# A graph-masked transformer block: the transposes in front of the MLP leave TensorE and take the way through 32x32 blocks and HBM

## The reference

```
nx = ln(x, ln1_g, ln1_b)
q, k, v = nx @ wq + bq, nx @ wk + bk, nx @ wv + bv        # 8 heads of 32
bias = where(adj > 0, 0.1 * adj * adj, -inf)
attn = softmax(q @ k.T / sqrt(32) + bias)                  # per head, 128x128
x1 = x + (attn @ v) @ wo + bo
n2 = ln(x1, ln2_g, ln2_b)
out = x1 + gelu(n2 @ w1 + b1) @ w2 + b2                    # 256 -> 1024 -> 256
```

## Time and profile before

| | |
|---|---|
| median of 3 runs | 1369.9 us |
| profiled execution, its own time | 1371.92 us |
| its span, first to last instruction | 1370.1 us |
| mean granted TensorE clock | 0.979 |
| PE, PEld busy | 97%, 84% |
| ACT, DVE, POOL busy | 84%, 83%, 47% |
| DMA | 155 GB/s, 212.80 MB |

### The profile page before, as it was taken

One profiled execution on the slowest core, in us unless ns is written; L12 is line 12 of the kernel. 1 busy time (PEld: TensorE's weight loads), 2 busy tenths in 40 slices (PEclk: granted clock), 3 DMA queues, 4 the chain that ended last, 5 costly groups with the idle time before them and its releaser, 6 DMA issues.

```text
span 1370.1 us, 33628 instructions
## 1 busy us (share of the span) xinstructions
PE 1333.6 (97%) x11364; PEld 1147.1 (84%) x11364; DVE 1140.7 (83%) x1971; ACT 1151.4 (84%) x3336; POOL 642.1 (47%) x615
## 2 busy tenths in 40 slices
PE   8579999999999999999999999999999999999999
PEld 7458888888888888888888888888888888888878
DVE  4789888888888888888888888888888888898762
ACT  4569888889888888988888988898988888898763
POOL 5634445554455554454555445555445455444110
PEclk7679999999999999999999999999999999999999
DMA  5355565455455545556545555554645654554330
GB/s 177 114 179 163 152 184 169 142 157 180 145 170 170 159 148 178 153 150 191 165 138 160 172 149 172 168 157 141 188 146 157 191 149 150 165 163 137 120 112 32
DMA packets 169587, 212.80 MB, mean 155 GB/s; under 512 B 16064, under 2 KB 148928, under 8 KB 169536
## 3 DMA queue, kind: packets, MB, share of 16 engines
q1 hardware_dynamic: 169536, 212.15, 50.7%
HBM read 111.95 MB, written 100.14 MB: 155 GB/s over the span
## 4 chain that ended last, share of the span: by engine, by line
PE 93%; DVE 2%; ACT 2%; DMA 1%; issue 1%; SPq 0%; POOL 0%; DVEq 0%; ACTq 0%
PE work L404 29%; PE work L405 25%; PE work L406 25%; PE area L461 6%; PE work L482 5%; PE work L519 2%; DMA probt<-moved_blocks 1%; PE work L411 0%; DVE soft L889 0%; DMA wa_raw<-in_L_gnn_wq 0%; ACT xhat L716 0%; DVE wa_raw L901 0%; DVE soft L865 0%; DVE w_lo L831 0%; DVE flat L982 0%
## 5 line engine op out<-in xcount | busy, mean ns | idle before, releaser
L647 ACT ACTIVATE soft<-soft,nmax 128x128 f32<-128x128 f32 x1024 | 396.7, 393 | 54.5 <-DVE nmax L873 54.1
L404 PE MATMUL work<-w_hi,hid_parts 128*128 128x256 f32 x1024 | 288.7, 282 | 0.5 <-DVE res L1001 0.5
L405 PE MATMUL work<-w_lo,hid_parts 128*128 128x256 f32 x1024 | 285.2, 279 | 0.0
L406 PE MATMUL work<-w_hi,hid_parts 128*128 128x256 f32 x1024 | 285.1, 278 | 0.0
L1100 POOL TENSOR_TENSOR xt_lo<-xraw,xt_hi 128x512 fp32r<-128x512 f32 x62 | 80.0, 1291 | 289.4 <-ACT xt_hi L681 289.4
L404 PE MATMUL work<-nt_hi,w_hi 128*128 128x512 f32 x512 | 207.5, 405 | 0.4 <-DVE nt_lo L966 0.4
L990 DVE TENSOR_TENSOR hid_parts<-late_memory,hid_parts 128x512 fp32r<-128x512 f32 x256 | 193.0, 763 | 14.3 <-ACT hid_parts L748 12.5
L738 ACT ACTIVATE late_memory<-work,b_col 128x512 f32<-128x512 f32 x256 | 174.4, 681 | 35.4 <-PE work L406 34.9
L405 PE MATMUL work<-nt_lo,w_hi 128*128 128x512 f32 x512 | 200.4, 391 | 0.0
L406 PE MATMUL work<-nt_hi,w_lo 128*128 128x512 f32 x512 | 200.0, 391 | 0.0
L404 PEld LDWEIGHTS work<-w_hi,hid_parts 128*128 128x128 f32 x1024 | 192.1, 188 | 5.5 <-DVE res L1001 0.7
(11 more groups left out here) (98 smaller groups left out, 3162.1 us busy)
## 6 DMA issues: line engine op xcount, KB each, us to landing
moved_blocks<-wa_raw SPq DMA_DIRECT2D x128, 512.0 KB, 2.9
probt<-moved_blocks SPq DMA_DIRECT2D x512, 128.0 KB, 3.0
xin<-in_x SPq DMA_DIRECT2D x32, 512.0 KB, 6.2
out<-res SPq DMA_DIRECT2D x128, 128.0 KB, 4.0
moved_flat<-flat SPq DMA_DIRECT2D x31, 512.0 KB, 3.0
xraw<-moved_flat SPq DMA_DIRECT2D x124, 128.0 KB, 3.5
adj_in<-in_adj SPq DMA_DIRECT2D x32, 256.0 KB, 3.1
res<-in_L_gnn_w SPq DMA_DIRECT2D x1, 1024.0 KB, 10.2
```

The source lines that it names most:

```text
L404: pe.matmul(o, lhs_hi, rhs_hi, start=first, stop=False)
L405: pe.matmul(o, lhs_hi, rhs_lo, start=False, stop=False)
L406: return pe.matmul(o, lhs_lo, rhs_hi, start=False, stop=last)
L647: a = act.activation(soft[:, b % 2, h, :], soft[:, b % 2, h, :], ACT.Exp, bias=nmax[:, b % 2, h:h + 1], accum_out=rsum[:, b % 2, h:h + 1])
```

## The change

The normalised rows of the second layer norm (`nhat`) now take the way of the first ones: DVE transposes them in 32x32 blocks into a second `flat` buffer, SP sends that to HBM and fetches it back in place of `nhat` (the name of this view is `nraw`), ACT makes `nt_hi` from it and POOL `nt_lo`. `flip` is gone from PE, and with it the two `nt` units of `UNITS`. For room, the rows of x that come back overwrite `xhat` instead of having an `xraw` of their own, so `norm1` of the next group waits for `taken["xt"]` and `norm2` for `taken["nt"]`. The identity, now used only at the start, lies in the second `flat` buffer until the first rows of `nhat` overwrite it.

The way through HBM takes time, so the MLP stands one step later: `up` of n-3 and n-4, `down` of n-4. All five bodies are in a new order. The diff, cut; the bodies' lists are shown below as instructions:

```diff
@@ UNITS: one row of each
-UNITS = [("v", 0, 0, 1), ("nt", 0, -2, 2), ("nt", 1, -2, 0), ("down", 2, -3, 1), ("down", 3, -3, 2),
+UNITS = [("mix", 3, -2, 3), ("qk", 0, 0, 0), ("up", 6, -4, 2), ("up", 7, -4, 1), ("proj", 3, -2, 3),
...
-PER_GROUP = {"down": GB, "v": 2, "qk": 4, "up": FC, "nt": DC, "mix": GB, "proj": GB}
-FIRST, EARLY, LATE = -2, 6, 2
+PER_GROUP = {"down": GB, "v": 2, "qk": 4, "up": FC, "mix": GB, "proj": GB}
+FIRST, EARLY, LATE = -1, 6, 1
+AHEAD = {"xt": 1, "nt": 0}
...
-        ident = sb("ident", [P, P])
-        xraw = sb("xraw", [P, GB * D])
-        flat = sb("flat", [P, RPB, GB * DC, HD])
+        flat = {k: sb(f"{k}_flat", [P, RPB, GB * DC, HD]) for k in ("xt", "nt")}
+        nraw = late_memory[:, 0:GB * D]
+        ident = flat["nt"][:, :, :, :].rearrange("p j m t -> p (j m t)")[:, 0:P]
+        xraw = xhat[:, :, :].rearrange("p b d -> p (b d)")
...
@@ SP
+            def fetch_flat(step, off, kind):
+                if not step.has(off) or kind == "xt" and step.at_first(off):
+                    return
+                raw = xraw if kind == "xt" else nraw
+                sp.wait_ge(flat_sent[kind], step.through(off - AHEAD[kind], 1, 0, 16))
                 for j in range(RPB):
+                    sp.dma_start(raw[j * HD:(j + 1) * HD, :].rearrange("p (i n) -> p i n", i=RPB),
+                                 moved_flat[kind][:, :, j, :].rearrange("i k n -> k i n")).then_inc(flat_landed[kind], 16)
...
@@ PE
-            def flip(step, off, c):
-                free(step, "nt", c)
-                for b in range(GB):
-                    if c == 0:
-                        pe.wait_ge(nhat_ready, step.through(off, GB, b))
-                    mm = pe.transpose(work[:, bank_of("nt", c), b * P:(b + 1) * P],
-                                      nhat[:, b, c * P:(c + 1) * P], ident[:, :])
-                mm.then_inc(full["nt"], 1)
...
@@ ACT
+            def flip_hi(step, off, kind, c):
+                dst, raw = (xt_hi, xraw) if kind == "xt" else (nt_hi, nraw)
...
+                if c == 0 and kind == "nt":
+                    need(act, full["up"], step.through(off - 1, FC, FC - 1))
+                act.wait_ge(flat_landed[kind], step.through(off - AHEAD[kind], 1, 0, LAND))
+                act.activation(dst[:, c, :].rearrange("p (b i t) -> p b i t", b=GB, i=RPB),
+                               raw.rearrange("p (i b c t) -> p b i c t", i=RPB, b=GB, c=DC)[:, :, :, c, :],
+                               ACT.Copy).then_inc(hi_taken[kind], 1)
...
-                    need(act, flat_ready, step.through(off - 2, 1, 0))
+                    need(act, taken["xt"], step.through(off - 1, DC, DC - 1))
...
-                    need(act, full["nt"], step.through(off - 1, DC, DC - 1))
+                    need(act, taken["nt"], step.through(off - 1, DC, DC - 1))
...
-                if not step.steady and step.n == 0:
+                if not step.steady and step.n == 1:
                     late_hi()
@@ DVE
-            def flip_lo(step, off, c):
-                dve.wait_ge(hi_taken["nt"], step.through(off, DC, c))
-                dve.tensor_tensor(nt_lo[:, c, :], work[:, bank_of("nt", c), :], nt_hi[:, c, :].bitcast(F32),
-                                  ALU.subtract).then_inc(taken["nt"], 1)
...
+            def flat_blocks(step, off, kind):
+                src, ready = (xhat, xhat_ready) if kind == "xt" else (nhat, nhat_ready)
+                need(dve, flat_sent[kind], step.through(off - 1 - AHEAD[kind], 1, 0, 16))
...
+                dve.transpose(flat[kind][:, :, :, :], src.rearrange("p b d -> p (b d)")
+                              .rearrange("p (m j k) -> p j m k", j=RPB, k=HD)).then_inc(flat_ready[kind], 1)
...
@@ POOL
+            def flip_lo(step, off, kind, c):
+                hi, lo, raw = (xt_hi, xt_lo, xraw) if kind == "xt" else (nt_hi, nt_lo, nraw)
+                pool.wait_ge(hi_taken[kind], step.through(off, DC, c))
+                pool.tensor_tensor(lo[:, c, :].rearrange("p (b i t) -> p b i t", b=GB, i=RPB),
...
```

More of the change, by code:

```diff
@@ L448, in _, with first_turn @@
                 pe.matmul(spare, ident[:, :], ident[:, :], start=True, stop=True)
+            def first_turn():
+                for c in range(DC):
+                    for b in range(GB):
+                        if c == 0:
+                            pe.wait_ge(xhat_ready, b + 1)
+                        mm = pe.transpose(work[:, c, b * P:(b + 1) * P], xhat[:, b, c * P:(c + 1) * P], ident[:, :])
+                    mm.then_inc(first_turned, 1)
+            early_columns()
+            first_turn()
             def score(step, off, b):
@@ L679, in rows_hi @@
                     return
-                act.wait_ge(flat_landed, step.through(off - 1, 1, 0, LAND))
-                act.activation(xt_hi[:, c, :].rearrange("p (b i t) -> p b i t", b=GB, i=RPB),
-                               xraw[:, :].rearrange("p (i b c t) -> p b i c t", i=RPB, b=GB, c=DC)[:, :, :, c, :],
-                               ACT.Copy).then_inc(hi_taken["xt"], 1)
-            def flip_hi(step, off, c):
-                if not step.has(off):
-                    return
-                if c == 0:
-                    need(act, full["up"], step.through(off - 1, FC, FC - 1))
-                act.wait_ge(full["nt"], step.through(off, DC, c))
-                act.activation(nt_hi[:, c, :], work[:, bank_of("nt", c), :], ACT.Copy)\
-                   .then_inc(hi_taken["nt"], 1)
+                act.wait_ge(flat_landed[kind], step.through(off - AHEAD[kind], 1, 0, LAND))
+                act.activation(dst[:, c, :].rearrange("p (b i t) -> p b i t", b=GB, i=RPB),
+                               raw.rearrange("p (i b c t) -> p b i c t", i=RPB, b=GB, c=DC)[:, :, :, c, :],
+                               ACT.Copy).then_inc(hi_taken[kind], 1)
             def query_key_copy(step, off, m):
@@ L750, in body @@
             def body(step):
+                hidden_hi(step, -4, 3)
+                attn_hi(step, -2, 3)
+                gelu(step, -4, 5)
+                hidden_hi(step, -4, 4)
+                hidden_hi(step, -4, 5)
+                gelu(step, -4, 6)
+                query_key_copy(step, 0, 0)
+                gelu(step, -4, 7)
+                hidden_hi(step, -4, 6)
+                hidden_hi(step, -4, 7)
+                exponential(step, -1, 2, 0)
+                flip_hi(step, -3, "nt", 0)
@@ L758, in body @@
+                gelu(step, -3, 0)
+                norm1(step, 1, 0)
+                norm1(step, 1, 1)
+                norm1(step, 1, 2)
+                norm1(step, 1, 3)
+                gelu(step, -3, 1)
+                norm2(step, -2, 0)
+                gelu(step, -3, 2)
+                norm2(step, -2, 1)
+                norm2(step, -2, 2)
+                attn_hi(step, -1, 1)
+                norm2(step, -2, 3)
+                values_copy(step, 0, 0)
                 exponential(step, 0, 0, 0)
-                attn_hi(step, -1, 1)
@@ L798, in body @@
+                hidden_hi(step, -3, 1)
+                hidden_hi(step, -3, 2)
+                values_copy(step, 0, 1)
+                flip_hi(step, 1, "xt", 0)
+                attn_hi(step, -1, 2)
+                flip_hi(step, 1, "xt", 1)
+                exponential(step, 0, 1, 0)
+                gelu(step, -3, 3)
+                gelu(step, -3, 4)
+                if not step.steady and step.n == 1:
                     late_hi()
@@ L974, in first_lo @@
                                       ALU.subtract).then_inc(taken["xt"], 1)
[L976 to L977 removed]
+            def flat_blocks(step, off, kind):
+                if not step.has(off) or kind == "xt" and step.at_first(off):
                     return
[L979 to L983 removed]
+                src, ready = (xhat, xhat_ready) if kind == "xt" else (nhat, nhat_ready)
+                need(dve, flat_sent[kind], step.through(off - 1 - AHEAD[kind], 1, 0, 16))
+                if kind == "nt":
+                    if step.at_first(off):
+                        dve.wait_ge(first_turned, DC)
+                    need(dve, taken["nt"], step.through(off - 1, DC, DC - 1))
+                dve.wait_ge(ready, step.through(off, GB, GB - 1))
+                dve.transpose(flat[kind][:, :, :, :], src.rearrange("p b d -> p (b d)")
+                              .rearrange("p (m j k) -> p j m k", j=RPB, k=HD)).then_inc(flat_ready[kind], 1)
             def hidden_lo(step, off, m):
```

282 lines of the change are left out of this document (113 added, 169 removed), and 3 rows, old and new, of the table UNITS.

## The result

The changed kernel takes 1345.7 us, the median of 4 runs (1345.3 to 1348.6), beside 1370.8 (1368.6 to 1372.0) for the kernel before on the same chip: a ratio of 0.983, interval 0.982 to 0.985. It is faster by 25.0 us; 33 were forecast. Its profiled execution took 1348.57 us, with a span of 1346.8 where 1334.5 was worked out.

The account below looks back on a forecast made before the run. PE's list was taken as the bound: a step of 40.56 - 0.96 - 0.48 = 39.1 us, group 31 at 1200 plus 134.3 gives span 1334.5; forecast 1337 us against the profiled 1371.9, range about 1327 to 1360.

Parts of the forecast that it names:

- flip 0 and 1 are eight matmuls ... 0.96: On PE, the eight transposing matmuls of `flip` 0 and 1 go, 0.96 us less a step.
- Two entries and three exits less ... 0.48: On PE, pairing small-tile stretches saves two entries and three exits at about 0.095 each, 0.48 us a step.
- ACT at 37.6 of the step, hidden: ACT, with two more table loads, is busy 37.6 us a step (37.2 to 38.5), under PE's 39.1.
- The rival by the page's drain: Each ACT table load also drains about 1380 ns: ACT needs 40.3 us a step, 1371, no change; chance 0.05.
- No wait in this has to end after PE. I take 39.1: Looped step: PE never waits for other engines' lists, so a step takes 39.1 us, ends 38.9 to 39.9.
- five narrow places: Looped step: `query_key` 0's bank, `mix` 3 behind `residual` 2, exponentials of sequence 1, rows of x, rows of `nhat`.
- DVE's pace in the fill: Before the looped steps DVE sets the pace: step 2 at 83, step 3 at 113, group 4 at 144.5 us.
- The drain: After `query_key` of group 31: 127.3 us of PE work, 4.3 of waits and 2.7 at the end, 134.3.
- The transfer of nhat hidden, the fill taking back 12 of 46: The HBM round trip of `nhat` delays nothing; the fill takes back 12 of 46 us from 32 shorter steps.
- The two large terms: PE's savings a step: 0.96 us for `flip`'s matmuls and 0.48 us for fewer borders of small tiles.
- small waits of PE: Rival: `mix` behind the residual, late banks, DVE-POOL conflicts or slow fill clock; 0.3 to 0.8 a step or 10 once; 0.24.
- the two cases: Whole time: PE at 39.0 to 39.3 a step, 1326 to 1346, chance 0.60; small waits, 1347 to 1362, 0.24.

## Why the prediction was right, step by step

- **"flip 0 and 1 are eight matmuls ... 0.96"**: right. 0.965 went, and putting eight like matmuls back cost 0.91.
- **"Two entries and three exits less ... 0.48"**: right; 0.51 by the trace, 0.46 lost when three pairs were taken apart, 0.22 won when one was made in the kernel before.
- **ACT at 37.6 of the step, hidden**: right; 37.5, and the step does not move when all loads go. Its room was 1.2 us where 1.5 was forecast: 2.8 us more made ACT the bound.
- **The rival by the page's drain**: excluded by the run with two more loads.
- **"No wait in this has to end after PE. I take 39.1"**: this step failed in its size, by 0.24. Of it 0.14 is `at_lo` behind a `hidden_lo` that stood for POOL, shown by moving it and by taking POOL's reads away. The forecast's five narrow places were laid out with DVE's durations taken alone, 0.69 for each subtraction, without the POOL instructions beside them. None of the five was the one that failed. The remaining 0.1 (the slower pitch of `down`, and `up` 0.06) is open.
- **DVE's pace in the fill**: step 2 was reached at 82.1 (83 forecast) and step 3 at 113.7 (113), both within a microsecond. Step 3 was 33.9 long where 31.5 was forecast; 1.8 of the 2.4 is the one normalise of 3.04. So group 4 came at 148.2 and not at 144.5. That DVE sets the pace there holds in the main; ACT has a part in it, since without its loads the fill is 3.6 shorter.
- **The drain**: right; with the clock at 1.00 throughout it was 134.2 to 134.4 with 127.8 to 128.0 of PE work (134.3 and 127.3 forecast). The 2.2 more of the changed kernel's own trace go with 3.4 us at the lower clock, in which a matmul of 512 columns took 0.42 and not 0.23. The forecast thought of the lower clock in the fill alone.
- **The transfer of nhat hidden, the fill taking back 12 of 46**: the first holds; of the second, fill and drain took about 15 by the half-length runs.

The two large terms were right to 0.03 us each, and so the sign and most of the size. Nearly all misses have one sign: each wait that the lists did not show made the time longer. The forecast had this as its "small waits of PE", and the result stands between the two cases, at the upper edge of the first.

## What to carry to other kernels

Where one engine is busy throughout, read its list start to start and price what leaves it, borders between kinds of work included; that sum holds, and what the other engines get costs nothing until one is about as full. Then lay the others' lists out with the durations that they have beside each other, not alone: a VectorE subtraction of two SBUF operands that meets one of GpSimd's large additions stands until that is done (2.73 us instead of 0.68 here), so nothing urgent should be behind it. And a longer pipeline pays a fixed price for a gain per step: here 15 us against 1.25 a step.

## What the runs showed of the hardware

- A row-tiled and a column-tiled stretch of 16 small matmuls cost 0.1 us on each outer side and nothing between them, whichever comes first.
- A DVE subtraction of 0.68 us took 2.73 beside a POOL addition of 2.41, a normalise of 1.22 took 3.04 beside one of 2.38; the engine shows no idle time in it. `add_edges`, which reads one operand from PSUM and one from SBUF, took 1.21 in all 31 places where it began beside a POOL subtraction. Beside POOL's power of 128x4 a two-operand subtraction kept its 0.68. The other way round, the POOL addition at 617.83, begun while a DVE subtraction ran, took 2.83, where the same addition took 2.36 at 113.11.
- A table load delays ACT by 1.30 us, and the first activation behind it starts 0.02 after its end.
- The first `query_key` of group 1 started anywhere from 41.0 to 46.0 us in the profiled runs of the changed kernel and its variants, and from 41.0 to 45.3 in five whose lists are the same on every engine up to there. It goes with the clock. The stretch from 20 to 40 us, in the changed kernel and in the run with `attn_lo` moved, by windows:

```profile
20.00:40.00 20.00, 18.50 (x124) 16.86 (x122) 8.11 (x12) 8.08 (x27) 6.51 (x6) 0.66 0.15 52
20.00:40.00 20.00, 14.16 (x129) 12.81 (x127) 11.45 (x15) 11.96 (x43) 8.45 (x8) 0.90 0.18 67
```

At 0.66 granted, PE is busy for 18.5 us of the 20 and group 1 starts at 44.9, at 0.90 for 14.2 and it starts at 41.0. The three variants that started at 41.0 to 41.4 had 12 us of the lower clock ahead of group 1, those that started at 44.4 to 46.0 had 19 to 24. What makes the clock differ between executions is open. It moves single times by up to 4 us, and it is why steps were compared here and not only totals.
